# Register loads of the adjacency tables in the first layer's edge loop: one register at a time and a pair of groups ahead, with the index list first in ScalarE's pair

## The reference, cut to what matters

```python
q, k, v = x @ Wq + bq, x @ Wk + bk, x @ Wv + bv
logits  = (q[dst] * k[src]) summed over each head's dimensions
a       = softmax of the logits over the edges of one dst
out     = segment_sum(a * v[src], dst)
```

## Time and profile before

| | |
|---|---|
| median of three runs | 6169.95 us |
| span of the profiled execution | 8199.2 us |
| first layer's edge loop in the profile (L1353 from 204.7 us, last sums at 1927) | 1723 us |
| gathers on GpSimd in it (L932) | 832, 986 ns each |
| granted TensorE clock in it | 0.71 of full |
| share of the span: PE, VectorE, GpSimd, ScalarE | 61%, 52%, 43%, 33% |

### The profile page before, as it was taken

How to read it: one execution, slowest core, us unless ns; L and a number is a source line. 1 busy time by engine, 2 the same in 40 slices (tenths; PEclk the granted TensorE clock), 3 DMA queues, 4 the chain that set the end, 5 groups by cost and what they waited for, 6 DMA issues and landing times. The chain is left out here.

```text
span 8199.2 us, 128493 instructions
## 1 busy us (share of the span) xinstructions
PE 5007.5 (61%) x25366; PEld 3730.4 (45%) x25375; DVE 4287.8 (52%) x10883; ACT 2730.0 (33%) x6600; POOL 3533.6 (43%) x3882
## 2 busy tenths in 40 slices
PE   2677777774888935555556345555555355655557
PEld 2555555553664524444444334444444244444443
DVE  6555555556664145555555545554556445555554
ACT  1333333333542003333334323333334133333342
POOL 2544444442320044555554445555552555555520
PEclk7676677776999965555556556555556555555568
DMA  2444444443444722222222122222221222222215
GB/s 72 128 137 135 137 134 139 134 137 86 134 134 158 249 54 58 64 62 62 65 59 61 42 54 63 62 59 66 60 63 35 54 60 61 60 60 61 58 35 202
DMA packets 579250, 728.81 MB, mean 89 GB/s; under 512 B 90091, under 2 KB 424769, under 8 KB 578686
## 3 DMA queue, kind: packets, MB, share of 16 engines
q0 software_dynamic: 123968, 282.81, 14.9%
q1 hardware_dynamic: 304800, 350.53, 14.5%
q10 hardware_dynamic: 149918, 88.82, 4.0%
HBM read 601.07 MB, written 120.75 MB: 88 GB/s over the span
## 5 line engine op out<-in xcount | busy, mean ns | idle before, releaser
L1769 POOL DMA_INDIRECT rows<-scratch_gat,index x2496 | 2437.4, 977 | 2757.1 <-DVE mix L1997 1461.9
L2103 PE MATMUL sums<-xr_part,hot_t 128*128 x7524 | 1106.9, 283 | 786.2 <-issue 466.9
L2158 PE MATMUL sums<-mix,vhot 128*128 128x128 f32 x4992 | 1261.8, 421 | 91.0 <-issue 81.7
L2103 PEld LDWEIGHTS sums<-xr_part,hot_t 128*128 128x128 bf16 x7524 | 775.5, 121 | 1102.7 <-issue 945.7
L2011 DVE TENSOR_TENSOR z<-sums,rows 128x512 f32<-128x512 f32 x624 | 428.7, 687 | 1563.0 <-remote 1425.4
L1836 ACT ACTIVATE moved_sums<-sums x624 | 373.1, 598 | 2620.8 <-remote 1599.0
L932 POOL DMA_INDIRECT rows<-scratch_kv,index_ring x832 | 820.6, 986 | 887.5 <-ACT index_ring L1242 661.3
L2158 PEld LDWEIGHTS sums<-mix,vhot 128*128 128x128 f32 x4992 | 1044.4, 303 | 186.6 <-issue 142.6
L1368 PE MATMUL sums<-at_hot,lo_hot 128*128 128x200 f32 x2496 | 820.1, 493 | 16.4 <-issue 11.2
L1826 ACT ACTIVATE vhot<-iota,edge_local 128x128 f32<-128x128 f32 x2496 | 791.2, 392 | 0.1
L2154 PE MATMUL sums<-zeros 128*128 128x8 bf16 x624 | 114.7, 184 | 999.9 <-issue 551.5
(11 more groups left out here) (514 smaller groups left out, 6385.9 us busy)
## 6 DMA issues: line engine op xcount, KB each, us to landing
piece<-scratch_adj SPq DMA_DIRECT2D x90, 1280.0 KB, 6.3
local_ring<-scratch_local_rows SPq DMA_DIRECT2D x633, 128.0 KB
scratch_spool<-rows ACTq DMA_DIRECT2D x208, 256.0 KB, 2.6
vals<-scratch_spool SPq DMA_DIRECT2D x208, 256.0 KB, 2.6
scratch_adj<-stage SPq DMA_DIRECT2D x25, 1600.0 KB
rows<-scratch_gat,index POOLq DMA_INDIRECT x2496
local_ring<-scratch_local_rows ACTq DMA_DIRECT2D x211, 128.0 KB
mask<-scratch_masks SPq DMA_DIRECT2D x234, 80.1 KB
```

The source lines that it names most:

```text
L1769: eng.indirect_dma_start(rows[:, slot, q, k * LINE:(k + 1) * LINE], None, table, bass.IndirectOffsetOnAxis(ap=index[:, slot, s:s + 1], axis=0)
L2103: ins = eng.matmul(B.ps[:, at + k * D:at + (k + 1) * D], hot_t[:, slot, k * P:(k + 1) * P], part[:, bass.ds(at_block, D)], start=(j == 0), ...
L2158: ins = eng.matmul(B.ps[:, bass.ds(of_block * D, D)], hot[:, v % MIXES, k * P:(k + 1) * P], mix[:, v % MIXES, k * D:(k + 1) * D], start=Fa ...
```

## The change

- TensorE's two loads at the head of a pair are gone. Five loads of one register each take their place, in the pair before: three from `pe_table` behind steps 0, 1 and 2 of the adjacency matmuls of the even group, two of block numbers behind steps 0 and 1 of the odd group. The first pair's are loaded ahead of the loop.
- ScalarE's load at the head of a pair is gone. Three loads of one register each follow the three `stage` activations of the odd group of the pair before.
- ScalarE now waits on `zed` and asks first; the field `need` and the wait on `room` come behind it, ahead of `fetch`.
- The tables are longer by one pair (A_TURN), for the loads past the end, and that part is set to zero. The values that are used are the same.

```diff
+    def fetch(self, at, n):
+        self.eng.load([self.regs[at]], self.B.blocks[0:1, bass.ds(n * GROUP, GROUP)].bitcast(I32))
+
+    def held(self, at):
+        return self.eng.snap(self.regs[at], min_val=0, max_val=(1 << 30) - 1)
...
-        self.pe_table = B.sb(ctx, "adj_pe_table", [1, A_STEPS], mybir.dt.uint8)
-        self.evac_table = B.sb(ctx, "adj_evac_table", [1, A_STEPS // 2], u16)
+        self.pe_table = B.sb(ctx, "adj_pe_table", [1, A_STEPS + A_TURN], mybir.dt.uint8)
+        self.evac_table = B.sb(ctx, "adj_evac_table", [1, (A_STEPS + A_TURN) // 2], u16)
...
+                eng.memset(A.pe_table[:, A_STEPS:], 0)
+                eng.memset(A.evac_table[:, A_STEPS // 2:], 0)
...
                 regs = [[eng.alloc_register(f"evac{B.fresh()}") for j in range(A_TURN // 4)] for h in range(pairs)]
+                need = eng.alloc_register(f"need{B.fresh()}")
+
+                def load_twos(pair, h, j):
+                    eng.load([regs[h][j]], A.evac_table[0:1, bass.ds(pair * (A_TURN // 2) + 2 * j, 2)].bitcast(I32))
...
                 make_hot_t(0, 0, 0, local_in[0].at(16))
+                for j in range(A_TURN // 4):
+                    load_twos(0, 0, j)
                 with eng.Fori(0, RING_TURNS) as i:
                     for q in range(RING_GROUPS):
                         n = i * RING_GROUPS + q
                         if q % 2 == 0:
-                            pair = i * (RING_GROUPS // 2) + q // 2
-                            eng.load(regs[q // 2], A.evac_table[0:1, bass.ds(pair * (A_TURN // 2), A_TURN // 2)].bitcast(I32))
-                            twos = [eng.snap(r, donate=True, min_val=0, max_val=(1 << 31) - 1) for r in regs[q // 2]]
-                            need = field(twos[0], NEED_FIELD.bit_length() - 1, 32, BLOCKS - 1)
-                            eng.wait_ge(room.sem, need + (room.at(0) + 1))
                             eng.wait_ge(zed.sem, zed.at((AHEAD + 2) * 2) + n * 2)
                             ask(n + AHEAD, (q + AHEAD) % RING_GROUPS)
+                            twos = [eng.snap(r, min_val=0, max_val=(1 << 31) - 1) for r in regs[q // 2]]
+                            eng.reg_alu(need, twos[0] // NEED_FIELD, 31, ALU.bitwise_and)
+                            eng.wait_ge(room.sem, eng.snap(need, min_val=0, max_val=BLOCKS - 1) + (room.at(0) + 1))
                         eng.wait_ge(off_made.sem, off_made.at(1) + n)
...
+                            if q % 2:
+                                load_twos(i * pairs + (q // 2 + 1), (q // 2 + 1) % pairs, k)
...
+                def load_slots(pair, h, j):
+                    eng.load([regs[h][j]], A.pe_table[0:1, bass.ds(pair * A_TURN + 4 * j, 4)].bitcast(I32))
+
+                def load_ahead(i, q, k):
+                    h = q // 2 + 1
+                    if q % 2 == 0 and k < A_TURN // 4:
+                        load_slots(i * pairs + h, h % pairs, k)
+                    if q % 2 == 1 and k < 2:
+                        blocks.fetch(2 * (h % pairs) + k, i * RING_GROUPS + 2 * h + k)
+                for j in range(A_TURN // 4):
+                    load_slots(0, 0, j)
+                for k in range(2):
+                    blocks.fetch(k, k)
                 with eng.Fori(0, RING_TURNS) as i:
                     for q in range(RING_GROUPS):
                         n = i * RING_GROUPS + q
                         if q % 2 == 0:
-                            pair = i * (RING_GROUPS // 2) + q // 2
-                            eng.load(regs[q // 2], A.pe_table[0:1, bass.ds(pair * A_TURN, A_TURN)].bitcast(I32))
-                            slots = [eng.snap(r, donate=True, min_val=0, max_val=(1 << 31) - 1) for r in regs[q // 2]]
-                            fours = blocks.load(q, 2, n)
+                            slots = [eng.snap(r, min_val=0, max_val=(1 << 31) - 1) for r in regs[q // 2]]
+                            fours = [blocks.held(q), blocks.held(q + 1)]
...
                             if k % 2:
                                 ins.then_inc(summed.sem, 1)
+                            load_ahead(i, q, k)
```

More of the change, by code:

```diff
@@ L1104, in _ @@
                 slot(tmp, bank, 1)
-                link(eng.scalar_tensor_tensor(out=A.pe_table[:, :], in0=tmp[:, 0:A_STEPS], scalar=16.0, in1=read[:, 0:A_STEPS],
+                eng.memset(A.pe_table[:, A_STEPS:], 0)
+                eng.memset(A.evac_table[:, A_STEPS // 2:], 0)
+                link(eng.scalar_tensor_tensor(out=A.pe_table[:, 0:A_STEPS], in0=tmp[:, 0:A_STEPS], scalar=16.0, in1=read[:, 0:A_STEPS],
                                               op0=ALU.mult, op1=ALU.add))
@@ L1125, in _ @@
                     scalar=float(NEED_FIELD), in1=by_turn[:, :, 0], op0=ALU.mult, op1=ALU.add))
-                link(eng.tensor_copy(A.evac_table[:, :], read[:, 0:n]))
+                link(eng.tensor_copy(A.evac_table[:, 0:n], read[:, 0:n]))
                 next_block = bounds[0:1, 0:BLOCKS * BLOCK_WINDOWS].rearrange("p (k j) -> p k j", j=BLOCK_WINDOWS)[:, 1:BLOCKS, 0]
@@ L1295, in _ @@
                         keep(n, q)
-                for r in sum(regs, []):
+                for r in sum(regs, []) + [need]:
                     eng.free_register(r)
```

## The result

The changed kernel takes 6229.99 us, the median of four runs (6222.09 to 6231.22), against 6170.01 for the kernel before beside it: a ratio of 1.0106, 95% interval 1.0085 to 1.0127. I forecast 6060 and a gain; it lost 60 us, and my range ended at 6190.

The account below looks back on a forecast made before the run. TensorE was taken to pace the loop, idled by its pair-head loads. 171 less 43 gave 128 us, plus 20 from ScalarE made 148, scaled to 111: 6170 to about 6060 us, range 5965 to 6190.

Parts of the forecast that it names:

- What bounds the kernel: In the loop, TensorE sets the pace, idled by issue (367.8 us) where its pair-head loads stand; gathers are not the limit.
- TensorE, what goes: At the pair's head, idle time of 1.65 us a pair behind the two table loads vanishes: 171 us in profile time.
- TensorE, what comes: Five single loads among the sums: three hidden in the even group, two costing in the odd group, 43 us.
- ScalarE: 20 us: ScalarE's way to the odd group's hot_t gets about 0.9 us shorter, saving 20 us of TensorE's waits, bounds 0 and 33.
- The index list: ScalarE's list for GpSimd's gathers comes over 1.2 us earlier in a pair, but nobody waits for gathers: nothing gained.
- The basis: Whole kernel: profiled span 1.329 times the median, so gains in profile time are scaled by 0.7525.
- the sum of 148 us: TensorE's net 128 us plus ScalarE's 20, in the profile's time; 111 scaled.
- Rival 2: Loads among the adjacency sums cost more, 0.70 us each at full clock: slower, 6268, or near 6220; chance 0.11.
- Rival 3: Issue breaks within even groups' L1353 matmuls come from the loads and go too: 148 us more, 5912; chance 0.07.

Follow-up runs that it names:

- e1_masked: The kernel before with only the field `need` held in a register by a mask, at its old place: 8186.05 us, 1.0007 of the kernel before.
- i1_after: The whole change run again, beside a kernel before in the slower condition: 8166.93 us against 8197.20, 0.9962.
- h3_no_block_loads: The change without the two block-number loads among the odd group's sums, in the slower condition: 8153.65 us, 0.9940 of the kernel before.
- f4_act_loads: The kernel before with ScalarE's three single loads, the ask still behind `need` and `room`, TensorE as before: 6171.87 us, 1.0006 of the kernel before.
- g1_singles_at_end: TensorE's five single loads all put behind the last sums of the pair, ScalarE as before: 6220.76 us, 1.0115 of the kernel before.
- f2_pe_only: TensorE's side of the change alone, five single loads among its sums, ScalarE as in e1_masked: 6305.31 us, 1.0216 of the kernel before.

## Why the prediction was wrong

**What bounds the kernel** was right near 6160: TensorE paces the loop, gathers do not (5.3 us of waits of z for them after the change), and the gap at the pair's head stood behind its loads.

**TensorE, what goes: 171 us.** The mechanism was right. That the size fits is luck. The term was in the profile's time, 129 us by the factor, and near 6160 131.5 us of issue went; but the factor had no ground. In the condition of its rows the idle time ahead of the q matmuls fell by 213 us (417.9 to 204.7). The mean of six pair starts also rests on two of them: the gaps of 3.19 and 2.23 us stand behind loads of 3028 and 2882 ns, not of 770. The last stands behind sums at half clock,

```profile
694.48 1.68 PE L1368 MATMUL sums<-at_hot,lo_hot 128*128 128x200 f32 x4
```

so a slow PE doesn't hide a load of 3 us, and a gap doesn't show that the sums before it ran at full clock, as I had read it for the next term.

**TensorE, what comes: 43 us.** This step failed; the runs show 226. I costed a load at 0.40 us with all around it, took the three of the even group for hidden, and gave the two of the odd group 0.42 us a pair. The odd group was the larger miss: its sums grew by 1.8 us a pair (2.8 to 4.6), and in the rows' own condition by 1.8 too (3.5 in `e1_masked`, 5.4 in `i1_after`, 3.9 in `h3_no_block_loads`, where only these two loads are gone). The even group's cover held in the condition where I read it (4.8 to 5.1 us, with 11% of the matmuls at full clock in both) and not near 6160 (3.9 to 4.6): in `f4_act_loads` 45% of its matmuls ran at full clock, in the change about 80%, so the 3.0 us of lead in the earlier trace rows were gone. I had named this loss of cover and priced it at 0.9 us a pair, but kept it out of the sum. What makes a load in the odd group dear: its mean was 0.52 us (109 us for 208 loads), not the 0.30 of the earlier trace rows, and a break isn't over with the load. The f32 sums of 332 ns back to back at full clock take 432 as the first behind a break, and odd sums that had run at full clock in 94% of their matmuls did so in 64 to 68% after. How the breaks bring the clock down is not shown. That the place makes the loss of the sums is shown: the same five loads outside them leave these at 847 us against 1065 (`g1_singles_at_end` and `f2_pe_only`).

**ScalarE: 20 us.** Near 6160 it is worth nothing alone (1.0006 and 1.0016) and 71 us beside TensorE's part; at 8182 it gained 52 us alone. I let it in as an addend, when near 6160 it is a bound that shows only once the other moved.

**The index list: nothing gained.** Right near 6160, where the ask alone even lost a little (1.0026), wrong at 8182, where it gained 119 us, and it is that condition that the rows came from. Why, stays open.

**The basis: 0.7525.** Wrong in kind. A profiled execution is no slower than another (6228.4 of span in 6230.21; 8189.3 in 8191.10). My rows showed another condition of the chip, and no factor leads from one to the other, since the same change gains 30 us there and loses 60 here. In its own condition the sum of 148 us met 30; the failed step above is the cause there too, with 217 in place of 43, while the 235 gained held more than the 171 of the pair's heads. That the sign came out there is luck, too.

**The rivals.** Rival 2 is what came: place (the sums), lever (the price of a load), and 6220 to 6268 as its time. Its turning point of 0.45 us a load, all around it included, was passed (0.47 bare, 0.53 with the address), but by its own sum 0.53 us costs 31 us, not 60; the rest is in the restart and the clock of the sums. I gave it 0.11 and let the range end at 6190, since I took the clock of 0.71 from the earlier trace rows for the kernel's own; near 6160 it is 0.84. Rival 3's breaks in the q matmuls of even groups are of the condition, not of the loads: `i1_after` still has 166.7 us of issue there, with no load ahead of them, and `f4_act_loads` had next to none behind the pair's head. Of TensorE's sequencer between q matmuls, the change near 6160, then near 8180 (ns min/median/max):

```profile
L1379 PEldq ALU_OP  x1664: 32/32/42, 197.8 to 1471.0; - x185
L1379 PEldq FUSED_REGOPS  x832: 89/123/144, 197.6 to 1470.7; - x167
```

```profile
L1379 PEldq ALU_OP  x1664: 3/32/728, 203.5 to 1893.7; - x185
L1379 PEldq FUSED_REGOPS  x832: 3/123/1412, 203.3 to 1893.4; - x167
```

The same program has register operations of up to 0.7 and 1.4 us in one condition and none over 0.15 in the other. They aren't from profiling, as I had thought. A small reading beside: by the earlier trace rows a second register adds 243 ns and a third 226, so the lower end of my 240 to 300 was too high.

## What to carry to other kernels

A load among busy instructions is hidden only as long as the engine's sequencer is further ahead of the engine than the load is long; ask at which clock that stretch runs once the gap is gone, not at which it ran before. Price it by the mean under load, and put a break's restart beside it. And where the span of a profile isn't near the median, don't scale it: find out first which of the two conditions the change will be judged in.

## What the runs showed of the hardware

One kernel had medians of 6152 to 6170 us or of 8026 to 8207, by the set of runs, and one chip showed both. In the slower condition TensorE's sequencer had over a thousand register operations of more than 0.5 us (1366 of 23166 in the profile of before), SyncE's over four hundred; in the faster one no such operation took more than 0.18 and 0.19 us (the change and `f4_act_loads`). The same edit, the ask alone, gained 1.5% in one and lost 0.3% in the other. A load of one register on TensorE took 294 ns at least and up to 1167 beside full gathers, with a mean of 0.47 us; on ScalarE its median was 281 ns. What lengthens them, and what sets the condition, no run here tells.
